# Self-attention scores of two units made in a row: four 32-row products, then two row maxima, instead of two and one

## The reference, cut to what matters

```python
def _fq(x, delta, zp, n_bits):
    xi = _round_ste(x / delta) + zp
    xq = jnp.clip(xi, 0.0, 2.0 ** n_bits - 1.0)
    return (xq - zp) * delta

def _attn(x, ctx, wq, wk, wv, wo, bo, dq, dk, dv, dw):
    q = (x @ wq).reshape(b, n, H, DH).transpose(0, 2, 1, 3)     # H = 16, DH = 32
    ...
    sim = jnp.einsum('bhid,bhjd->bhij', _fq(q, dq, 128.0, 8), _fq(k, dk, 128.0, 8)) * SCALE
    attn = jax.nn.softmax(sim, axis=-1)
    out = jnp.einsum('bhij,bhjd->bhid', _fq(attn, dw, 0.0, 8), _fq(v, dv, 128.0, 8))
...
x = _attn(h1, h1, ...) + x          # self-attention: the part that is changed
x = _attn(h2, context, ...) + x
x = a * jax.nn.gelu(g, approximate=False) @ ff_w2 + ff_b2 + x
```

## Time and profile before

| | us |
|---|---|
| median of 3 executions | 3563.54 |
| lowest, highest | 3556.68, 3568.96 |
| profiled execution, its own time | 3564.55 |
| its span in the trace | 3562.7 |
| mean granted TensorE clock | 0.909 of full |
| PE busy in the span | 84% |
| DVE, ACT, POOL busy | 62%, 47%, 42% |

### The profile page before, as it was taken

How to read it: one execution, slowest core, us unless ns; L and a number is a source line. 1 busy time by engine, 2 the same in 40 slices (tenths; PEclk the granted TensorE clock), 3 DMA queues, 4 the chain that set the end, 5 groups by cost and what they waited for, 6 DMA issues and landing times.

```text
span 3562.7 us, 50726 instructions
## 1 busy us (share of the span) xinstructions
PE 2979.5 (84%) x19712; PEld 2166.1 (61%) x19712; DVE 2193.1 (62%) x3543; ACT 1670.1 (47%) x2678; POOL 1506.3 (42%) x1165
## 2 busy tenths in 40 slices
PE   5467677798788889899887989889887888898899
PEld 5345545456576756656666755656766655655777
DVE  2263596785464587587564587587464588588421
ACT  4223275584333275376333276376323267277221
POOL 2364254465454154354364254354363345254221
PEclk9688856799899989899999999999999999999999
DMA  6934302234452312323452322232443321331434
GB/s 189 325 143 136 121 4 101 78 113 178 146 180 83 142 66 96 134 86 127 138 181 92 137 74 96 97 122 84 165 155 115 136 81 66 119 131 72 154 142 165
DMA packets 200621, 442.68 MB, mean 124 GB/s; under 512 B 95040, under 2 KB 103488, under 8 KB 182464
## 3 DMA queue, kind: packets, MB, share of 16 engines
q1 hardware_dynamic: 187968, 437.83, 34.3%
q10 hardware_dynamic: 12416, 1.62, 0.3%
HBM read 369.67 MB, written 65.54 MB: 122 GB/s over the span
## 4 chain that ended last, share of the span: by engine, by line
PE 52%; DVE 22%; POOL 9%; ACT 8%; issue 5%; DMA 3%; SPq 1%; ACTq 1%; POOLq 0%; DVEq 0%
PE psum L1685 15%; PE psum L1686 14%; PE psum L1687 14%; DVE mx L1565 8%; DVE w1T L1584 4%; PE psum L1967 3%; POOL w_lo L873 3%; ACT e L1256 2%; PE psum L1955 2%; DVE den L1571 2%; POOL x L885 1%; ACT psum L1146 1%; PE psum L1981 1%; DMA fw_lo<-pieces 1%; ACT ht_hi L1145 1%
## 5 line engine op out<-in xcount | busy, mean ns | idle before, releaser
L940 POOL TENSOR_SCALAR w1b<-e,rec 128x1024 f16<-128x1024 f32 x512 | 574.7, 1122 | 731.8 <-DVE rec L1573 534.7
L1565 DVE TENSOR_REDUCE mx<-psum 128x1 f32<-128x1024 f32 x512 | 622.4, 1217 | 36.5 <-PE psum L1956 36.4
L1256 ACT ACTIVATE e<-psum,nb,scale 128x1024 f32<-128x1024 f32 x512 | 617.5, 1206 | 16.8
L1685 PE MATMUL psum<-h_hi,fw_hi 128*128 128x512 f32 x1024 | 465.3, 454 | 17.8 <-DVE h_lo L1349 9.0
L1686 PE MATMUL psum<-h_lo,fw_hi 128*128 128x512 f32 x1024 | 417.8, 408 | 0.0
L1687 PE MATMUL psum<-h_hi,fw_lo 128*128 128x512 f32 x1024 | 416.4, 407 | 0.0
L1584 DVE TENSOR_SCALAR w1T<-psum 128x1024 bf16<-128x1024 f16 x512 | 348.7, 681 | 94.3 <-PE psum L1967 89.4
L1967 PE MATMUL psum<-ident,w1b 128*128 128x128 f16 x4096 | 351.0, 235 | 64.7 <-DVE w1T L1584 61.8
L1967 PEld LDWEIGHTS psum<-ident,w1b 128*128 128x128 f16 x4096 | 260.1, 105 | 233.4 <-issue 197.8
L1685 PE MATMUL psum<-w_hi,ht_hi 128*128 128x512 f32 x640 | 266.8, 417 | 72.7 <-DVE e L1502 42.3
L1439 DVE TENSOR_TENSOR x<-psum,x 128x512 f32<-128x512 f32 x224 | 152.3, 685 | 260.3 <-PE psum L1687 259.9
(11 more groups left out here) (180 smaller groups left out, 6125.1 us busy)
## 6 DMA issues: line engine op xcount, KB each, us to landing
fw_hi<-pieces SPq DMA_DIRECT2D x168, 512.0 KB, 3.3
fw_lo<-pieces SPq DMA_DIRECT2D x168, 512.0 KB, 4.3
w_hi<-kept SPq DMA_DIRECT2D x48, 1024.0 KB, 4.8
w_lo<-kept SPq DMA_DIRECT2D x48, 1024.0 KB, 7.9
mixed<-mixed SPq DMA_DIRECT2D x32, 1024.0 KB, 4.9
fbias<-in_fside_Bx16xSxS SPq DMA_DIRECT2D x64, 256.0 KB, 3.0
unsplit<-in_L_xattn_ff_w SPq DMA_DIRECT2D x24, 512.0 KB, 5.2
pieces<-fw_hi SPq DMA_DIRECT2D x24, 512.0 KB, 2.6
```

The lines of the kernel that those rows point to most:

```text
L940: pool.tensor_scalar(w1b[u % NH][:], e1[u % NE][:], rec1[:, u % 8:u % 8 + 1], HALF, ALU.mult, ALU.add).then_inc(w1_ready.sem, 1)
L1256: act.activation(e1[s % NE][:], psum[:, i:i + 2, :].rearrange("p i n -> p (i n)"), ACT.Exp, bias=nb1[:, s % 4:s % 4 + 1], scale=scale[:, 0:1],
L1565: dve.tensor_reduce(mx1[:, s % 4:s % 4 + 1], psum[:, i:i + 2, :].rearrange("p i n -> p (i n)"), AX, ALU.max).then_inc(maxed1.sem, 1)
L1685: pe.matmul(o, s_hi, m_hi, start=first, stop=False)
```

## The change

Slots of even number now do the products and the maxima of two units, s and s+1, and slots of odd number do neither. On PE both units' waits for free banks come first, then the four products in a row: heads 0 and 1 (or 2 and 3) lie on the quarters 0, 2, 1 and 3 (or 2, 0, 3 and 1) of the rows, so that no two of the four share a quarter. On DVE the two maxima follow each other, and the reciprocals come after them. Nothing else is edited. ACT, POOL and SP have the same lists as before; the banks, buffers and the lag of five slots are the same, and so is the number of instructions that compute. From the second edit on the new kernel's lines are three higher (L1955, L1956, L1967, L1981 become L1958, L1959, L1970, L1984).

```diff
@@ DVE, self_attention @@
-                    if s < UNITS:
-                        wait_filled(dve, ("s1", n, s))
-                        i = bank_of(("s1", n, s))
-                        dve.tensor_reduce(mx1[:, s % 4:s % 4 + 1], psum[:, i:i + 2, :].rearrange("p i n -> p (i n)"),
+                    for u in (s, s + 1) if s < UNITS and s % 2 == 0 else ():
+                        wait_filled(dve, ("s1", n, u))
+                        i = bank_of(("s1", n, u))
+                        dve.tensor_reduce(mx1[:, u % 4:u % 4 + 1], psum[:, i:i + 2, :].rearrange("p i n -> p (i n)"),
                                           AX, ALU.max).then_inc(maxed1.sem, 1)
@@ PE, self_attention @@
-                    if s < UNITS:
-
-                        hg, t, h = s // 16, s // 4 % 4, s % 4
-                        wait_empty(("s1", n, s))
-                        i = bank_of(("s1", n, s))
-                        if s < 2:
-                            wait_bank(i + 1, ("s1", n, s))
+
+                    for u in (s, s + 1) if s < UNITS and s % 2 == 0 else ():
+
+                        wait_empty(("s1", n, u))
+                        if u < 2:
+                            wait_bank(bank_of(("s1", n, u)) + 1, ("s1", n, u))
+                    for u in (s, s + 1) if s < UNITS and s % 2 == 0 else ():
+
+                        hg, t, h = u // 16, u // 4 % 4, u % 4
+                        i = bank_of(("s1", n, u))
                         p = slice(DH * h, DH * h + DH)
                         turned = slice(DH * (h ^ 2), DH * (h ^ 2) + DH)
                         pe.matmul(bank(i), q1[n % NC][p, hg, t * P:t * P + P], k1[0][p, hg, :], start=True, stop=True)
                         ins = pe.matmul(bank(i + 1), q1_turned[turned, hg, t * P:t * P + P], k1[1][turned, hg, :],
                                         start=True, stop=True)
-                        done(ins, ("s1", n, s))
+                        done(ins, ("s1", n, u))
```

## The result

The changed kernel takes 3785.68 us (median of 4, 3781.82 to 3792.86) against 3564.76: 1.0625 times as long, with a 95% interval of 1.060 to 1.065. That is +221 us where 181 were forecast, and slower, as forecast. The profiled execution took 3792.86 us, the slowest of the four; its span is 3791.1, 228.4 longer than before.

What follows compares the result with a forecast made beforehand. Before, DVE or PE was fullest, by stage; after, a 4.88 us chain through both exponentials was to bound each pair. Terms 33 + 57 + 55 + 15 + 15 + 6 = +181 on 3564.5 gave 3745 us, range 3680 to 3805.

Steps and rivals of the forecast that it cites:

- no period under 4.88 us: Self-attention stages: from first maximum to first maximum a pair takes at least 4.88 us at the 2.4 GHz clock.
- chunk 0: Stage without guests: transposes waiting for `w1T` make pairs take 5.10 and 5.59 us in turn; 165.9 against 132.3, +33.
- PE's saving: One set of products per pair leaves its place on PE: 0.21 us saved, at most 0.32, priced at nothing.
- the chain itself: Loop from a pair's products through first maximum and both exponentials to the next products: 4.88 us, 151.3 per 31 pairs.
- ACT's work between the exponentials: Guest work between a pair's exponentials counts fully: 24.6 us in chunk 1, 8.7 in 2, 4, 6, 19.6 in 3, 5, 7.
- DVE's guest work and the clock: Guest operations behind an odd slot's `w1T` delay the next maximum, +15; PE idling at gelus lowers its clock, +6.
- The link from the exponential to the products: Second exponential's start at 444.53 to PE's restart on the banks it freed at 445.88, within the 4.88 us a pair.
- bank 4: PE's transposes wait for `w1T` after both maxima, delaying next products: pairs of 5.10 and 5.59 us in chunk 0, elsewhere nothing.
- the fourth rival: Clock stays at 1.2 GHz for a fifth of the seven hosted stages' pairs: 87 us more, 3830; chance 0.13.
- The first: PE is the bound and saves 0.21 to 0.32 us a pair: 3510, down to 3483; chance 0.04.
- The second: Chain met half-way: hosted stages lose little, only chunk 0 its 33 us: near 3600; chance 0.03.
- the third: ACT's work between exponentials partly covered, only gelus count: 3692; chance 0.14 for 3600 to 3700.

Runs made afterwards that it cites:

- The control: Kernel before the change, with ACT's guest work of both slots of a pair put behind the second exponential: 3579.9 us, ratio 1.0043.

## Why the prediction was right, and by how much it was short

The mechanism held in the main points that the profile can show: maxima in twos; no period under 4.88 us (the shortest is 4.95) in 248 pairs; chunk 0 at 167.8 us for 165.9 and in turn 5.2 and 5.6 us a pair; the loss in these stages alone; PE's saving swallowed by idle time. Two signs came out weaker: the second exponential holds the products in 207 of 248 pairs, not in nearly all, and chunks 2 and 3 take 171.5 and 179.6 us where 160 and 171 were forecast. The sum, +181, was short by a fifth of what was measured. Term by term, in us, for the eight stretches of 31 pairs:

| term | forecast | measured |
|---|---|---|
| chunk 0 | 165.9 | 167.8 |
| chunks 1 to 7: the chain itself, 217 pairs at 4.88 and at 4.97 | 1059 | 1078.5 |
| ACT's work between the exponentials | 109.5 | 110.3 |
| DVE's guest work and the clock: maximum late behind the products | 21 | 26.6 |
| products late behind transposes or values | none | 22.6 |
| table load ahead of the first exponential of chunks 2, 4 and 6 | none | 3.8 |
| sum of these | 1355 | 1409.6 |
| sum of the stretches by the trace | | 1408.3 |
| less the 1173.7 of before | +181 | +235 |
| outside the stretches | 0 | -6 |

The measured terms are differences of the start times in the trace, link by link over all pairs: the median link for the chain, what the two exponentials stand apart beyond 1.51 for ACT's work, what lies beyond 0.43 from the products to their maximum for the fourth line and beyond 1.44 from the second exponential to the products for the fifth.

- *The link from the exponential to the products* was read as 1.35 us in a place where PE waits for one bank's semaphore. Behind two waits it is 1.44. With each wait ahead of its own products it is 1.35 again. 0.09 us over the 217 pairs of chunks 1 to 7 is 20 us, the one error that a reading of the earlier trace rows could not show.
- *DVE's guest work and the clock* were priced at 15 + 6, and nearly so they came out. In 38 pairs of chunks 1 to 7 the maximum starts late with a guest's operation of DVE (L1439 or L1476) between it and the second `w1T`, 16.7 us in all. In 30 pairs it starts late with DVE idle and the products at the 1.2 GHz level, 6.5 us. The rest of the 26.6 is shared or smaller. The granted clock of chunks 1 to 7 fell from between 0.92 and 0.95 to between 0.89 and 0.92, so the fourth rival's mechanism is there, in a small size.
- *Products late behind transposes or values* is the term that the sum lacked: with guests it had put bank 4 at nothing. POOL's bias is about 10 of the 22.6 us, and its price of 3.2 to 4.1 us a stage stood in the trace of before. The other 12 lie in pairs in which the transposes and values end after the second exponential, those behind a gelu among them; they were not taken apart further.
- *The table load* of 1.28 us stands in the first pair of chunks 2, 4 and 6, in the kernel before too; the chain of 4.88 for every pair left it out.
- *ACT's work between* was sized within 1 us in all: 26.9 us in chunk 1, 8.5 in each of chunks 2, 4 and 6 and 19.3 in each of 3, 5 and 7, for 24.6, 8.7 and 19.6. The control shows the cause: moved behind, it gives 75 us, and only in the changed kernel.
- *PE's saving* was taken as 0.21 us a pair of 0.32 at most. The products of the second unit start with the first ones, not 0.11 us later, and the guest's matmul comes as early as behind two, so the full 0.32 was saved where the clock is at its 2.4 GHz level. PE's busy time in the stretches fell by 1048.32 - 993.63 = 54.7 us, which is 0.22 a pair; what took the rest back was not looked into. It bought nothing, as priced.
- *The rivals.* The first (PE bound, faster) needed PE's work of a pair above 4.88 us; it is 138.91 / 31 = 4.48 in chunk 3. DVE, whose share the prediction held against this rival, is busy only 1029.64 of 1408.33 us after, so it is the wait for both pairs of banks and not DVE's load that keeps the gain out. The second would have needed a shorter link, and the third that ACT's small operations were hidden; they are not, as the 110.3 shows.

## What to carry to other kernels

Two buffers that are refilled together are one buffer: before work is batched across a pair, add up the loop from the first fill through both consumers and back, and compare it with what a pair takes now. Everything on a consumer's list between the two halves then counts in full, though it was free before, and so moving that work behind the second half is the first thing to try. Where a batch has two sides, one in the filler's order and one in the reader's, test each alone: here either half was worse than both.

## What the runs showed of the hardware beyond what was expected

- Four products of 32 rows and 512 columns on the four quarters of the rows start within 0.01 us of each other and release PE for the next matmul after 0.33 us, where two do after 0.32: the second pair costs PE 0.01 us. In the one place of the old trace where four stood in a row, the second two came 0.11 us later.
- With two semaphore waits ahead of them the products start 0.09 us later after the exponential that they wait for (1.44 us from its start, the median of every chunk, against 1.35 in the kernel with each wait by itself, the median of chunks 1 to 7). In the trace of chunk 5 the wait that ends last is then an instruction of its own on PE's queue (EVENT_SEMAPHORE, 0.05 us), and the matmul starts 0.11 us after the start of that instruction; with each wait by itself it is the weight load that waits, and the matmul starts less than 0.01 us after that.
- A DVE operation of two columns took up to 4.13 us, and ended with POOL's addition of 2048 columns; with that addition in four pieces it took at most 1.24 us under one of them.
